# Semilinear gradient steps: maxima and sums on VectorE, one exponential on ScalarE instead of eight

## What is computed

```python
for _ in range(2):
    Wc = jnp.concatenate([W_in, W_out], axis=2)
    Kc = jnp.concatenate([kch, vch], axis=2)
    Vc = jnp.concatenate([vch, kch], axis=2)
    attn = jax.nn.softmax(jnp.einsum('bqhd,bkhd->bhqk', Wc, Kc) * scale, axis=-1)
    G = jnp.einsum('bhqk,bkhd->bqhd', attn, Vc)
    G_out, G_in = jnp.split(-G, 2, axis=2)
    W_in = W_in - lrch[:, :1, :, :1] * G_in
    W_out = W_out - lrch[:, :1, :, 1:] * G_out
```

## Time and profile before

| | us |
|---|---|
| median of 3 runs | 1219.69 |
| lowest and highest | 1217.71, 1220.15 |
| the profiled execution | 1217.85 |
| its span, first to last instruction | 1216.1 |
| busy TensorE, VectorE, ScalarE, GpSimd (of the span) | 87%, 67%, 41%, 26% |

### The profile page before, as it was taken

One profiled execution on the slowest core, in us unless ns is written; L12 is line 12 of the kernel. 1 busy time (PEld: TensorE's weight loads), 2 busy tenths in 40 slices (PEclk: granted clock), 3 DMA queues, 4 the chain that ended last, 5 costly groups with the idle time before them and its releaser, 6 DMA issues. The chain is left out here.

```text
span 1216.1 us, 18598 instructions
## 1 busy us (share of the span) xinstructions
PE 1061.4 (87%) x6220; PEld 787.6 (65%) x6220; DVE 813.3 (67%) x1592; ACT 494.7 (41%) x954; POOL 320.2 (26%) x265
## 2 busy tenths in 40 slices
PE   5993999999999963698999999999999987875997
PEld 4883566666666652477878776968696876763443
DVE  4565286778778883357888787979688876633332
ACT  1220255776676774134444443434252534310110
POOL 0344376677577662000000000000000000011553
PEclk9997898989889975788999999999899987765999
DMA  4281410222021000100010101010010031046541
GB/s 153 87 333 59 82 42 1 59 58 57 2 58 35 18 18 32 56 1 35 1 53 1 53 2 54 1 53 2 2 53 1 18 105 70 36 159 261 158 144 58
DMA packets 59924, 75.12 MB, mean 62 GB/s; under 512 B 37758, under 2 KB 42302, under 8 KB 57792
## 3 DMA queue, kind: packets, MB, share of 16 engines
q1 hardware_dynamic: 52384, 53.05, 13.7%
q0 software_dynamic: 5152, 12.59, 3.2%
q10 hardware_dynamic: 2304, 8.39, 1.7%
HBM read 56.71 MB, written 22.81 MB: 65 GB/s over the span
## 5 line engine op out<-in xcount | busy, mean ns | idle before, releaser
L1196 POOL COPY fw_x<-fw_x 128x1024 f32<-128x1024 f32 x8 | 8.3, 1040 | 536.0 <-DMA xh_scr<-fw_x 502.4
L556 POOL TENSOR_TENSOR aw_wtent<-aw_tent,aw_e 128x1760 f32<-128x1760 f32 x32 | 100.7, 3145 | 114.1 <-DVE aw_e L552 114.1
L745 PE MATMUL aw_psum_kv<-all_xWv,aw_c 128*128 128x512 f32 x256 | 124.6, 633 | 0.0
L528 POOL TENSOR_TENSOR aw_tent<-all_const,all_ix 128x1760 f32<-128x1760 f32 x32 | 100.6, 3145 | 5.1 <-POOL aw_wtent L556 4.6
L851 ACT ACTIVATE aw_cT<-aw_psum_av 32x256 f32<-32x256 f32 x128 | 80.5, 629 | 38.7 <-PE aw_psum_av L774 37.6
L733 PE MATMUL aw_psum_kv<-aw_c,all_xWk 128*128 128x352 f32 x256 | 81.6, 474 | 9.5 <-POOL aw_A L632 9.5
L2020 PE MATMUL ex_psum_y<-ex_We,ex_gT 128*128 x184 | 85.0, 607 | 0.0
L745 PEld LDWEIGHTS aw_psum_kv<-all_xWv,aw_c 128*128 128x128 f32 x256 | 49.4, 203 | 52.9 <-issue 51.1
L539 DVE TENSOR_TENSOR aw_prod<-aw_tent,aw_psum_s 128x1760 f32<-128x1760 f32 x32 | 63.5, 1984 | 23.8 <-ACT aw_tent L534 17.3
L1510 PE MATMUL fw_psum_front<-all_xWo,fw_cT 128*128 128x512 f32 x128 | 66.0, 666 | 11.7 <-DMA fw_cT<-c_scr 11.4
L733 PEld LDWEIGHTS aw_psum_kv<-aw_c,all_xWk 128*128 128x128 f32 x256 | 49.0, 196 | 35.2 <-POOL aw_A L632 9.6
(11 more groups left out here) (265 smaller groups left out, 2256.7 us busy)
## 6 DMA issues: line engine op xcount, KB each, us to landing
ex_We<-expert SPq DMA_DIRECT2D x1, 8192.0 KB, 22.4
aw_craw<-ctx SPq DMA_DIRECT2D x8, 704.0 KB, 4.8
xh_scr<-fw_x SPq DMA_DIRECT2D x10, 512.0 KB, 3.6
pj_x<-x_tok SPq DMA_DIRECT2D x8, 512.0 KB, 3.6
q_scr<-pj_QT ACTq DMA_DIRECT2D x8, 512.0 KB, 2.9
aw_Qb<-q_scr SPq DMA_DIRECT2D x32, 128.0 KB, 3.4
c_scr<-aw_cT ACTq DMA_DIRECT2D x8, 512.0 KB, 2.7
fw_cT<-c_scr SPq DMA_DIRECT2D x8, 512.0 KB, 4.8
```

Of the source, the lines that this page charges most:

```text
L528: return nc.gpsimd.tensor_tensor(self.tent[r][:], bc(rows, 1, self.nu * NK), bc(ix, 2, self.wr), ALU.subtract)
L556: return eng.tensor_tensor(self.wtent[:], self.tent[r][:], bc(self.e[:].rearrange("p u k -> p (u k)"), 2, self.wr), ALU.mult)
L745: mm = nc.tensor.matmul(ps_kv[:, j % 2, :], rows, Wv[:, c, :], start=(c == 0), stop=(c == KC - 1))
```

## The change

In `maxima` VectorE no longer scales the maxima; it subtracts them from all of `at`, 128 x 1024. ScalarE takes one exponential of 128 x 1024 with a constant scale, without bias and without sums. In `normalise` VectorE sums `at` by rows before it takes the reciprocal. `LINKS`, the number of waits of VectorE on its own results in a group, grows by one for each of the two steps.

```diff
-LINKS = (1 + 4) + (2 + 4) + 2 * 4
+LINKS = (1 + 4) + (2 + 4) + 2 * 5
...
-                ch.link(nc.vector.tensor_reduce(atop[:], at[:].rearrange("p j g n -> p (j g) n"), AX, ALU.max))
-                nc.vector.tensor_scalar(atop[:], atop[:], -ATT_SCALE, None, ALU.mult).then_inc(s_done.sem, 1)
+                by = at[:].rearrange("p j g n -> p (j g) n")
+                ch.link(nc.vector.tensor_reduce(atop[:], by, AX, ALU.max))
+                nc.vector.tensor_tensor(by, by, bc(atop[:], 2, P), ALU.subtract).then_inc(s_done.sem, 1)
...
                 dve.wait_ge(a_done.sem, a_done.at(t.r, it + 1))
+                ch.link(nc.vector.tensor_reduce(asum[:], at[:].rearrange("p j g n -> p (j g) n"), AX, ALU.add))
                 ch.link(nc.vector.reciprocal(asum[:], asum[:]))
...
                 act.wait_ge(s_done.sem, s_done.at(i, it + 1))
-                for n in range(S2):
-                    mm = nc.scalar.activation(at[:, n // KC, n % KC, :], at[:, n // KC, n % KC, :], ACT.Exp,
-                                              bias=atop[:, n:n + 1], scale=ATT_SCALE, accum_out=asum[:, n:n + 1])
-                mm.then_inc(a_done.sem, 1)
+                nc.scalar.activation(at[:], at[:], ACT.Exp, scale=ATT_SCALE).then_inc(a_done.sem, 1)
```

## The result

The changed kernel takes 1232.06 us (median, 1231.42 to 1235.55), the kernel before, run beside it, 1219.14. The ratio is 1.0125, with a 95% interval of 1.0093 to 1.0157: slower by 1.25%. The forecast was 1233 with a range of 1225 to 1246. The profiled execution took 1231.65 us with a span of 1229.5, against 1216.1 before: 13.5 us more before rounding, where the sum had 13.0.

The account below looks back on a forecast made before the run. The prediction took VectorE's chain in each group's second half as the bound, TensorE having no cover for it. Terms: 5 x 1.64 + 2 x 1.2 = 10.6, plus 2.35 in group 7, 13.0 on 1219.7: given as 1233, range 1225 to 1246.

Parts of the forecast that it names:

- The place of the cost: Groups 0 to 6: first steps cost 0, second steps delay VectorE's chain up to the group boundary, by 1.64 us.
- The first-step cover: First steps of groups 1 to 6: VectorE's idle 0.99 us at z1 and 1.70 us before the reciprocal hide the added work.
- The prices of the operations: In each step: exponential 1.1 us on ScalarE, sum 1.22 us and subtraction 1.225 us on VectorE.
- The price of a boundary: End of second steps: TensorE about 1.2 us late at `sk1`, 1.64 us at `sc0`; 1.2 us at back edges.
- Group 7: Last group: first step +1.25 us, second +1.15 us of which TensorE feels 1.1, together 2.35 us.
- The sum of 13.0: Whole kernel: 10.6 us from the group boundaries plus 2.35 us from the last group, 13.0 us slower.
- The clock rival: Five boundaries without back edge: new TensorE idle time lowers the granted clock, 7 to 15 us more, 1240 to 1248; chance 0.18.
- a slow sum: VectorE's sum takes 1.98 us in every step, adding 8.6 us: 1241; chance 0.05.
- all on the path: All 16 steps: VectorE's added 2.27 us each counts in full, 36 us: 1256; chance 0.04.
- a gain for earlier rows: First steps: rows 0.45 us earlier let groups go on earlier, gaining 3.6 us: with absorption 1217 or less; chance 0.05.
- Hidden after all: Second steps: slack behind the second maxima exceeds 1.64 us, only the last group pays 2.35 us: 1222.0; chance 0.08.

Follow-up runs that it names:

- the run with three extra operations: Kernel before with three unread 128x1024 VectorE operations added in each first step, between causal products and reciprocal: ratio 1.0153.
- the single exponential alone: Kernel before with one 128x1024 exponential, no subtraction or sum on VectorE, reciprocal of a constant: ratio 0.9999.
- the written-out pair: Kernel before and changed kernel, each with the loop over groups written out on every engine: ratios 0.9915 and 1.0069 against the kernel before.
- two products: Changed kernel with two unread 128x512 matmuls on TensorE ahead of each back edge: ratio 1.0085; the same on the kernel before: 0.9988.
- the sum alone: Kernel before with VectorE summing the rows and eight exponentials keeping their bias but not their sums, in both steps: ratio 1.0088.
- the extra operation in the second step: Kernel before with one more 128x1024 VectorE operation in each second step, between rates_add and the reciprocal: ratio 1.006.
- the subtraction alone: Kernel before with VectorE subtracting the maxima from all of at, eight exponentials keeping their sums without bias, both steps: ratio 0.9997.

## Why the prediction was right, point by point

**The place of the cost: shown.** In groups 0 to 6 first steps cost nothing and second steps carry all of it, and more time on VectorE, with nothing else changed, is enough for such a cost. What it explains is the 1.40 us at line 1293, not the 0.32 us behind line 172. The first-step cover held as worked out: the wait of 0.99 us at z1 is gone, in group 2 the sum starts after 0.15 us and the reciprocal comes 8.80 us behind the first maxima, where it came 9.18: 0.38 earlier, 0.45 forecast, and worth nothing, as the run with the first step alone shows.

```profile
690.67 2.48 DVE L1328 TENSOR_TENSOR fw_qk<-fw_psum_back,all_const 128x512 f32<-128x512 f32 x4 [1.25 <-PE fw_psum_back L1559]
693.30 1.22 DVE L1356 TENSOR_REDUCE fw_asum<-fw_at 128x8 f32<-128x1024 f32 x1
694.55 0.20 DVE L1357 RECIPROCAL fw_asum<-fw_asum 128x8 f32<-128x8 f32 x1
```

**The prices of the operations: right.** The exponential 1.057 us for 1.1, the sum 1.216 for 1.22, the subtraction 1.225 as its twin. The Trainium skill, "VectorE: DVE Perf Modes", section "Rules for kernel authors", by which a `tensor_reduce` is the slowest operation of the engine, is not borne out for a reduction with 8 results: 1.216 beside 1.225 us.

**The price of a boundary: 1.71 us for 1.64, by two errors that offset.** The slack on the way was larger than forecast, so that 1.40 us arrive at line 1293 and not 1.64; and 0.32 us came on top at line 172, which nothing in the trace of before announced. The size of the total is in that part luck. The path was right but not the sizes on it: TensorE's wait at `sk1`, which was to be about 1.2 us, is 0.37 us (`sk1` begins 0.87 us later), and 0.19 us stand at `vt0`, which the sum had not named. At a back edge without a fall the second half is 43.10 us in the changed kernel. The kernel before has none without a fall; the run with three extra operations, whose second step is that of the kernel before, has 41.82 there, as has the single exponential alone. That is +1.28, forecast 1.2.

**Group 7: right in its first terms, hidden in the span.** The wait of TensorE for the first normalised rows grew from 4.48 to 5.66 us (+1.18, forecast 1.25), and from the second maxima to the products with `win` it is 13.86 us for 12.75 (+1.11, forecast 1.1):

```profile
1024.49 1.97 PE L1505 MATMUL fw_psum_back<-all_const,fw_at 128*128 128x128 f32 x8 [5.66 <-DVE fw_at L1363]
...
1048.81 1.16 PE L1489 MATMUL fw_psum_back<-fw_win,fw_kT 128*128 128x128 f32 x8 [0.38 <-DVE fw_win L1339]
```

But the first half of group 7 grew by only 0.46 us, as TensorE ran part of it at a higher clock than before: the products with `win` of the first step took 1.16 us for 1.88, and its wait before them was 1.58 us for 2.07. In the written-out pair the half grew by 1.85 (24.50 for 22.65), there with a lower clock than in the kernel before.

**The sum of 13.0: right in size, in part by luck.** The 13.5 us of the two spans are: start of group 0 +1.6 (559.1 for 557.5, ahead of any changed instruction; over all kernels of this study it lies between 554.3 and 559.1), first halves of groups 0 to 7 together -0.55, second halves of groups 0 to 6 +9.88, the rest behind the last second maxima +2.57, of which 1.11 are the term above. Of the second halves 1.37 + 1.72 + 1.73 + 1.06 us are price (the last, group 6, with a low clock in both kernels), 3.41 is price and a fall at the boundary of groups 3 and 4, and the two back edges are +2.40 and -1.80: before, the clock fell at both, after, at one.

**The clock rival: real, and given too little weight.** It was put as five boundaries with 1.5 to 3.1 us each, or none. What happens is in between: of the boundaries without back edge up to that of groups 5 and 6, in kernels that carry the whole change, 1 of 4 (changed kernel), 1 of 4 (with two products) and 2 of 6 (written out) have a fall, of 1.7 us each. With the second step alone 2 of 4 have one, with the sum alone 1 of 4, with the extra operation in the second step 0 of 4: in all 7 of 26 boundaries of kernels in which line 1293 comes 0.37 us or more later. In the other eight kernels it is 0 of 34. The stage view at the one of the changed kernel:

```profile
798.00:802.00 4.00, 4.00 (x7) 1.62 (x6) 3.40 (x10) 0.80 (x2) 0.00 (x0) 0.59 0.00 0
```

Ahead of it TensorE has gaps of 0.37 and 0.19 us, the same as in group 1 (shown above) and group 5, where the clock held; before, there was one of 0.11 us. With the sum alone the fall came behind gaps of 0.19 and 0.13 us. By the Trainium skill, "TensorE: Matmul & The Clock Gate", section "A second HAM failure mode: psum-queue depth-cycling", small gaps can be enough; with 7 of 26 the traces agree that they can and not that they do each time. No run put in gaps without a later VectorE, so that the gaps are the cause is argued from these counts. Which boundary is hit looks like chance, and I can't say what decides it. Added over the loop of the changed kernel it is 1.7 us in its profile. The plain price is 4 x 1.71 + 2 x 1.28 + 1.06 + 2.3 = 12.8 us; by medians the three pairs are 12.9, 14.0 and 18.6 us apart. The changed kernel itself had, in its profile, fewer falls at the back edges than the one before, which pays for the one in the middle; why they were fewer, no run shows.

**The rival of a slow sum, of all on the path, of a gain for earlier rows: out.** The prices and the run with the first step alone exclude them. "Hidden after all" decides, as it said, by the slack behind the second maxima; this is 0.9 us where the sum had taken off 0.65, which hides the subtraction with shorter exponentials but not the sum.

## What to carry to other kernels

Ask of work that is moved between engines where the receiving engine has a wait, not how much room its busy share leaves: the same 2.3 us were free in one step and cost 1.4 to 1.7 in the next. The delay is shortened only by the waits between the place of the change and the engine that is waiting (here 0.9 us), so each part of a change is to be followed to that engine. A delay that reaches a fully busy TensorE can cost more than itself: in 7 of 26 boundaries with gaps of a few tenths of a microsecond the clock fell, for another 1.7 us. And a short loop's back edge may be the larger prize: writing it out gained 0.85%, more than anything that was tried on the exponentials.

## What the runs showed of the hardware

- **The price of a back edge.** At full clock a group with a back edge of this loop takes 1.9 to 2.0 us more than one without (64.38 and 64.49 for 62.48); in the changed kernel the second half takes 1.4 us more (43.10 for 41.66). With 1.9 us of TensorE work put in ahead of it, 0.70 and 0.93 us of idle time stayed behind that work, 0.30 and 0.36 in the changed kernel, and with 3.6 us none.
- **Idle time without a releaser on VectorE.** In the looped kernels with a later VectorE (the change, the sum alone, the extra operation) one instruction of line 172 or its neighbour starts 0.2 us late with "issue" as the reason, three times in the loop, and 0.32 us arrive at the next maxima. The subtraction alone and the second step alone did not have it, nor had the groups of the written-out pair as a rule. The cause is open.
- **The price of a bias and of sums on ScalarE.** Eight activations of 128x128 without a bias from memory took 0.29 us each where those with one took 0.39. Leaving out the sums left each at 0.386 us but took the step from 3.2 to 2.45 us (the sum alone). Leaving out the bias with the sums kept took it to 2.45 us too (the subtraction alone).
- **Two readers of SBUF.** In the run with three extra operations, these met GpSimd's copy of x. In five groups both took longer: up to 1.942 us for 1.226, and 1.92 to 2.04 us for the copy, which else takes 1.04. Their ends lie as if one went after the other. In each of the five, the operation that had begun before the copy kept its 1.22 to 1.23 us, the copy ended 0.90 us behind it, and the next operation ended 1.08 us behind the copy. Where the copy began first, in the two groups after them, it kept its 1.04 us and the operation took 1.69 and 1.53.

```profile
L1358 DVE TENSOR_TENSOR fw_idle<-fw_idle x24: 1224/1226/1942, 562.3 to 1030.4; 128x1024 f32<-128x1024 f32 x24
```

```profile
626.67 1.92 POOL L1197 COPY fw_x<-fw_x 128x1024 f32<-128x1024 f32 x1 [128.11 <-DMA xh_scr<-fw_x]
```

In the changed kernel the sum runs beside the same copy, and both keep their time (1.22 us from 693.30, above, and the copy):

```profile
693.47 1.04 POOL L1196 COPY fw_x<-fw_x 128x1024 f32<-128x1024 f32 x1 [62.97 <-DMA xh_scr<-fw_x]
```

The Trainium skill, "SBUF — State Buffer", section "Who interferes with whom", says that a VectorE instruction with two inputs in SBUF contends with a GpSimd instruction that reads SBUF, and that a reduction never does. These rows agree with both.
